# First attention stage of a two-layer kernel: matmul groups reordered within each item, smaller transposes, value projection and result normalisation moved

## What is computed

```python
t = xn.reshape(Bb, Cc, WS, n1, WS, n2).transpose(0, 3, 5, 2, 4, 1)
tok = t.reshape(Bb * n1 * n2, WS * WS, Cc)                 # 49 tokens of 64 channels
qk = (tok @ qk_w.T).reshape(-1, WS * WS, 2, HEADS, DH)
q = qk[:, :, 0].transpose(0, 2, 1, 3)
k = qk[:, :, 1].transpose(0, 2, 1, 3)
attn = softmax(einsum('bhqd,bhkd->bhqk', q, k) * scale, axis=-1)
v = relu(tok @ v_w.T).reshape(-1, WS * WS, HEADS, DH).transpose(0, 2, 1, 3)
o = einsum('bhqk,bhkd->bhqd', attn, v)
...
x = x + _L0_conv_ref(_gn(x), ...)     # first attention
x = x + _L1_conv_ref(_gn(x), ...)     # 5x5 neighbourhood attention and a projection
```

## Time and profile before

| | |
|---|---|
| Median of 3 runs | 1735.7 us (1733.81 to 1741.63) |
| Span of the profiled execution | 1743.6 us; its own launch time is not given |
| First attention in it | 26.05 to about 775 us |
| PE / DVE / ACT / POOL busy | 82% / 80% / 59% / 65% of the span |
| One unit in the loop, 450.00 to 461.01 us | 11.01 us |
| Mean granted TensorE clock | 0.924 |

### The profile page before, as it was taken

One profiled execution on the slowest core, in us unless ns is written; L12 is line 12 of the kernel. 1 busy time (PEld: TensorE's weight loads), 2 busy tenths in 40 slices (PEclk: granted clock), 3 DMA queues, 4 the chain that ended last, 5 costly groups with the idle time before them and its releaser, 6 DMA issues.

```text
span 1743.6 us, 62829 instructions
## 1 busy us (share of the span) xinstructions
PE 1434.3 (82%) x26281; PEld 755.6 (43%) x26281; DVE 1396.1 (80%) x1964; ACT 1030.6 (59%) x1861; POOL 1139.6 (65%) x873
## 2 busy tenths in 40 slices
PE   4989999999999999974597888879797786966754
PEld 2656666666666666651132332323233232322332
DVE  4774777777777777778999999999989999995933
ACT  3554777777777777754564747667474766543300
POOL 5333555555555555530679999999999999985700
PEclk9775999999999999987699999999999999997978
DMA  8702011111104220215202324223232522126079
GB/s 330 301 11 52 18 34 39 28 46 24 50 17 100 21 55 18 55 33 141 52 20 59 98 52 122 52 73 91 58 79 51 122 52 71 39 67 244 22 309 388
DMA packets 106870, 152.35 MB, mean 87 GB/s; under 512 B 71362, under 2 KB 83650, under 8 KB 100034
## 3 DMA queue, kind: packets, MB, share of 16 engines
q1 hardware_dynamic: 106690, 149.67, 29.4%
HBM read 77.99 MB, written 65.20 MB: 82 GB/s over the span
## 4 chain that ended last, share of the span: by engine, by line
PE 44%; DVE 18%; POOL 16%; issue 13%; ACT 5%; SPq 1%; DMA 1%; DVEq 0%; POOLq 0%; ACTq 0%
POOL arena L799 11%; PE PS L1484 7%; PE PS L1321 7%; PE PS L1330 5%; PE PS L1346 5%; DVE arena L1111 4%; PE PS L1298 4%; POOL arena L810 4%; PE PS L1290 4%; DVE arena L1107 4%; PE PS L1507 3%; PE PS L1428 3%; PE PS L1309 2%; PE PS L1360 2%; ACT arena L988 2%
## 5 line engine op out<-in xcount | busy, mean ns | idle before, releaser
L1220 DVE TENSOR_TENSOR arena<-arena,PS 128x1568 f32<-128x1568 f32 x334 | 583.9, 1777 | 16.1 <-PE PS L1484 8.3
L799 POOL TENSOR_TENSOR arena<-arena 128x1568 f32<-128x1568 f32 x168 | 517.7, 3123 | 87.7 <-PE PS L1428 68.1
L765 POOL TENSOR_TENSOR arena<-arena,consts 128x196 f32<-128x196 f32 x512 | 294.3, 609 | 283.7 <-ACT arena L849 283.7
L1484 PE MATMUL PS<-arena,consts 32*32 32x392 f32 x12800 | 396.9, 512 | 78.3 <-DVE arena L1220 23.4
L997 ACT ACTIVATE PS<-arena 128x392 f32<-128x392 f32 x334 | 166.3, 501 | 255.8 <-DVE arena L1220 255.1
L1428 PE MATMUL PS<-arena,consts 128*32 128x392 f32 x1664 | 200.3, 554 | 83.2 <-POOL arena L799 42.1
L1107 DVE TENSOR_REDUCE arena<-PS 128x8 f32<-128x392 f32 x256 | 143.2, 559 | 144.7 <-PE PS L1321 143.2
L1484 PEld LDWEIGHTS PS<-arena,consts 32*32 32x32 f32 x12800 | 145.8, 104 | 246.0 <-issue 96.1
L874 ACT ACTIVATE arena<-PS 128x512 f32<-128x512 f32 x256 | 152.9, 597 | 161.0 <-PE PS L1330 157.2
L810 POOL TENSOR_TENSOR arena<-arena 128x1568 f32<-128x1568 f32 x66 | 202.7, 3081 | 29.4 <-ACT arena L937 20.7
L1330 PE MATMUL PS<-consts,arena 128*128 128x128 f32 x1024 | 177.9, 299 | 0.2
(11 more groups left out here) (109 smaller groups left out, 1724.2 us busy)
## 6 DMA issues: line engine op xcount, KB each, us to landing
arena<-x_wide_dram SPq DMA_DIRECT2D x32, 660.0 KB, 8.2
arena<-x_wide_dram SPq DMA_DIRECT2D x256, 67.5 KB, 2.0
x_wide_dram<-arena SPq DMA_DIRECT2D x12, 1125.0 KB
arena<-in_x_dram SPq DMA_DIRECT2D x8, 1568.0 KB, 14.5
x_wide_dram<-arena SPq DMA_DIRECT2D x64, 196.0 KB, 4.3
x_dram<-arena SPq DMA_DIRECT2D x8, 1568.0 KB, 7.5
attn_dram<-arena SPq DMA_DIRECT2D x256, 49.0 KB, 3.0
arena<-x_dram SPq DMA_DIRECT2D x8, 1568.0 KB, 19.0
```

Of the source, the lines that this page charges most:

```text
L765: i = nc.gpsimd.tensor_tensor(k_bd[k][:, r], keys.unsqueeze(1).to_broadcast([P, HEADS_T, S]), head_mask.unsqueeze(2).to_broadcast([P, HEAD ...
L799: nc.gpsimd.tensor_tensor(tile, x_part, by, ALU.mult).then_inc(pool_tile, 1)
L1220: nc.vector.tensor_tensor(by_channel(v_tiles[n % V_RING]), shifted_values(half, k), over_channels(PS[:, 2 + n % W_BANKS, 0:PIX]), ALU.mult ...
L1484: mm = nc.tensor.matmul(PS[dst, 4 + i, 0:PIX], ident[src, src], tile[src, c * PIX:(c + 1) * PIX], start=done == 0, stop=done == NK - 1)
```

## The change

Seven edits, all in the first attention:
1. PE: within an item, QK is issued right behind S. V moves from items 1 and 2 to items 0 and 1 and stands behind T, as do Tv and To. So the 64x64 groups stand together, then all 128x128 groups, then W. `await_project` (the wait for tokens) moves from item 1 to item 0, ahead of V.
2. PE: W is issued as three heads, then the waits for keys and subtraction, then the fourth head. The fourth head is now all that lies between these waits and the next S.
3. T and To take 113 rows and give 113 columns (`ROWS = SP + S = 64 + 49`) instead of 128. Tv keeps 128. `probs_T` is set to ones once, by POOL.
4. ACT: `copy_transposed` copies 4 x 113 columns instead of 512.
5. ACT: `copy_v` moves from item 3 to item 2, ahead of the first `copy_qk`, also for unit 0; `gather` moves from item 2 to item 3, behind the second `copy_qk`.
6. DVE: `normalise` stands ahead of `subtract_max` and works on item n-3 instead of n-2.
7. The counts waited for on `proj_copied` follow the new order of the copies.

```diff
+ROWS = SP + S
@@ POOL
+            for t in probs_T:
+                nc.gpsimd.memset(t, 1.0)
@@ POOL, unit
-                        pool.wait_ge(proj_copied, 3 * u + k // 2 + 1)
+                        pool.wait_ge(proj_copied, 3 * u + k // 2 + 2)
@@ ACT, copy_transposed
-                nc.scalar.activation(probs_T[k % 2].rearrange("p j n -> p (j n)"), PS[:, 7, :],
+                nc.scalar.activation(probs_T[k % 2][:, :, 0:ROWS], PS[:, 7, :].rearrange("p (j n) -> p j n", j=4)[:, :, 0:ROWS],
@@ ACT
             gather(0, 0)
+            copy_v(0, 0)
             for b2 in range(2):
                 copy_qk(0, 0, b2)
-            copy_v(0, 0)
             gather(1, 1)
@@ ACT, unit
                     elif not last:
+                        if k == 2:
+                            copy_v(u + 1, 1 - up)
                         copy_qk(u + 1, 1 - up, k - 2)
-                    if k == 2 and not (isinstance(u, int) and (u == STATS_UNIT or u + 2 >= UNITS)):
+                    if k == 3 and not (isinstance(u, int) and (u == STATS_UNIT or u + 2 >= UNITS)):
                         gather(u + 2, up)
-                    if k == 3 and not last:
-                        copy_v(u + 1, 1 - up)
@@ DVE, unit
+                    if not (first and k < 3):
+                        normalise(n - 3, (k - 3) % 4, up if k >= 3 else 1 - up)
                     subtract_max(n, k)
-                    if not (first and k < 2):
-                        normalise(n - 2, (k - 2) % 4, up if k >= 2 else 1 - up)
@@ PE, transpose_v
-                pe.wait_ge(proj_copied, 3 * u + 3)
+                pe.wait_ge(proj_copied, 3 * u + 1)
@@ PE, transpose_probs
-                    i = nc.tensor.transpose(PS[:, 7, j * P:(j + 1) * P],
-                                            probs[k][:, 2 * j:2 * j + 2, :].rearrange("p h s -> p (h s)"), ident)
+                    i = nc.tensor.transpose(PS[:, 7, j * P:j * P + ROWS],
+                                            probs[k][0:ROWS, 2 * j:2 * j + 2, :].rearrange("p h s -> p (h s)"),
+                                            ident[0:ROWS, 0:ROWS])
@@ PE, unit
                     scores(n, k, up)
-                    if not (first and k < 2):
-                        await_values(n - 2, 2 * u + m % 2 + 1 - (0 if k >= 2 else 2))
-                    if k == 1 and not last:
-                        await_project(u + 1)
+                    if k in (1, 2) and not last:
+                        project_qk(1 - up, k - 1)
                     if not (first and k == 0):
                         transpose_probs(n - 1, (k - 1) % 4)
-                    if not (first and k < 2):
-                        weigh_values(n - 2, m, up if k >= 2 else 1 - up)
-                    if k in (1, 2) and not last:
-                        project_qk(1 - up, k - 1)
+                    if k < 2 and not last:
+                        if k == 0:
+                            await_project(u + 1)
+                        project_v(1 - up, k)
+                    if k == 0:
+                        transpose_v(u, up)
...
                     if k == 3 and not first:
                         await_output(u - 1)
+                        transpose_output(1 - up)
+                    if not (first and k < 2):
+                        await_values(n - 2, 2 * u + m % 2 + 1 - (0 if k >= 2 else 2))
+                        weigh_values(n - 2, m, up if k >= 2 else 1 - up, range(3))
                     if not (last and k == 3):
                         pe.wait_ge(kbd_ready, n + 2)
                         pe.wait_ge(sub_done, n + 1)
-                    if k == 0:
-                        transpose_v(u, up)
-                    elif k in (1, 2) and not last:
-                        project_v(1 - up, k - 1)
-                    elif k == 3 and not first:
-                        transpose_output(1 - up)
+                    if not (first and k < 2):
+                        weigh_values(n - 2, m, up if k >= 2 else 1 - up, range(3, 4)).then_inc(pv_done, 1)
```

More of the change, by code:

```diff
@@ L1158, in _ @@
             units(dve, unit, peel=PEEL)
-            normalise(4 * UNITS - 2, 2, 1)
-            normalise(4 * UNITS - 1, 3, 1)
+            for k in range(1, 4):
+                normalise(4 * UNITS - 4 + k, k, 1)
             order_tokens(UNITS - 1, 1)
@@ L1339, in await_values, with weigh_values @@
                     pe.wait_ge(norm_done, n)
-            def weigh_values(n, k, up):
+            def weigh_values(n, k, up, heads=range(4)):
                 b2, e = k // 2, k % 2
-                for j in range(4):
+                for j in heads:
                     for r in range(2):
```

7 lines of the change are left out of this document (4 added, 3 removed).

## The result

The changed kernel takes 1668.8 us (median of 4 runs, 1667.39 to 1670.86), beside 1738.1 us for the kernel before (4 runs, the three behind 1735.7 and one more, 1733.81 to 1741.63): a ratio of 0.960, 95% interval 0.956 to 0.964. The forecast was 1700, the range 1678 to 1724.

The account below looks back on a forecast made before the run. In the loop PE alone bound items 1 and 2, a loop through DVE items 3 and 0. Loop -30, slow-clock stretches -7 and start-up +1.3 made -36 us: 1735.7 - 36 = 1700, range 1678 to 1724.

Parts of the forecast that it names:

- PE's sums: PE's own work in the loop's items 0 to 3: 2.45, 2.34, 2.01, 2.07; 8.87 us a unit instead of 10.1.
- rival 1: Transposes and matmuls of the same shape don't join, in items 1 and 0: 18 us, giving 1718; chance 0.15.
- It costs nothing while DVE is free: On DVE, normalise (0.53 us) fits into the 0.69 in which DVE used to wait for S.
- Item 2, 2.50: In the loop, item 1's statistics delay normalise and the reduction to S2 + 0.96, so item 2 takes 2.50 us.
- The ACT chain, 5.60: In items 3 and 0, exponentials, second copy_qk and gather hold back V, so S3 to S1 takes 5.60 us.
- Hidden under it: Moved copy_v makes the next unit's keys late, S0 at S3 + 2.63 instead of 2.22; PE waits for gather anyway, no cost.
- Rival 3: V is not late: items 3 and 0 take 5.08 us, 28 us less, giving 1672; chance 0.08.
- The slow-clock stretches, 6.7 us: Before 177 us, two 41 us stretches at clock 0.50 hold 2.68 units instead of 2.36: 6.7 us gained in all.
- the start-up cost: In unit 0 the first keys also wait for V and copy_v: some 1.3 us once, bounds 0 and 2.
- the other units before 177 us: Held by DVE's statistics and the arriving images, they gain nothing (bounds 0 and -5).
- what would make it wrong: An ACT chain no row shows, or another number of slow-clock stretches before 177 us, some 10 us either way.
- Rival 4: The clock falls in the loop, each slow stretch costing 13 us; five give 1765; chance 0.07 (above 1744).

Follow-up runs that it names:

- a_norm_old: The changed kernel with DVE's old order put back, subtract_max first and then normalise of item n-2: 1739.5 us.
- a_gather2: The changed kernel with gather back behind the first copy_qk in item 2 instead of last in item 3: 1653.1 us.
- a_g2_qkfirst: The changed kernel with gather back in item 2 and also the first copy_qk ahead of copy_v: 1637.1 us.
- b_again: The kernel before, unchanged, profiled once more: 1736.8 us in its one run.

## Why the prediction was wrong, point by point

- *PE's sums:* right. S with QK, T with V, W and the step of 113 columns came within 0.02 us, and T and V at 0.88 exclude rival 1.
- *"It costs nothing while DVE is free":* right, and it is what the change stands on; a_norm_old puts 0.94 us a unit on it. I had not said that the new PE list is worth nothing without it.
- *Item 2, 2.50:* mis-sized, measured 2.25 to 2.27. I added lengths of records (0.88 and 0.29) where the next instruction starts 0.1 earlier. The rows had it: the two copies from 452.76 have a record of 0.87, and the reduction behind them starts at 453.48, 0.15 ahead of its end. Another 0.04 is the 0.65 that I took from the reduction to the subtraction. 53 x 0.24 = 13 us.
- *The ACT chain, 5.60:* right as a mechanism (a_gather2), 0.11 too long, 6 us. Here I took the 0.47 between copy and `gather` for ACT's time.
- *"Hidden under it", the late keys:* right; in the changed kernel they cost nothing, and 16 us came out when the chain had been cut (a_g2_qkfirst).
- *Rival 3 (V not late, 1672):* the measured time is near its figure, but by another way; V is late.
- *The slow-clock stretches, 6.7 us:* the step that failed. I kept their number and length (two of 41 us) and only let more work fit into them. Measured, one of 13.7 us is left, and unit 10 starts 31.5 us earlier, 26 more than the forecast; the start-up cost, 1.27 us (unit 0 starts at 27.32 instead of 26.05), was right. Some 20 of the 26 are this term. The other 6 are the other units before 177 us, which I had put at nothing (bound -5). This split is an estimate from the units that run at full clock on both sides: unit 1 takes 10.82 us instead of 11.68, units 8 and 9 take 10.44 and 9.91 instead of 11.19 and 11.04 in b_again. In "what would make it wrong" the stretches stood as "some 10 us either way", too little: two stretches with 2.36 units each at 17.4 instead of 11 us are 15 us apiece. Why the stretches got short is open, as said above. And the profile before was one with much slow clock: in b_again, the same kernel, unit 10 starts 12 us earlier.
- *Rival 4 (the clock falls in the loop):* didn't come; T and To, eight transposes in a row in item 3, run at full clock (PEclk 1.00 over 535 us). The Trainium skill's sentence that the full clock doesn't engage for transposes (TensorE: Matmul & The Clock Gate, Part 4) isn't borne out by this trace.
- The terms that were off add up: 13 + 6 + 26, less 3.6 lost after the attention, is 41 us, and 36 + 41 = 77 stands against the 76 us between the two spans. That the medians lie only 69 apart fits the many slow stretches of the profile before.

## To carry to other kernels

Cost the next instruction on an engine from start to start, never by the length of the record ahead of it. A slow clock in the trace of before is not a fixed item: if PE is saturated in it, ask whether the changed list would let it come back, and put its whole price into the range. And of a bundle of moves, test each the other way round: here the new list on PE pays only with the late normalise, and the late `gather`, the early `copy_v` and the early V together cost 41 us of what the rest had gained, 32 of them by the order on ACT.
